# Cross-attention with eight heads and a mixture of experts on one core: another order of the attention steps on four engines

## Chip, cores and metric

The kernel runs on one core of a Trainium2 chip. The metric is the device time of one execution in microseconds (us). The kernel before was run three times: 2055.81, 2058.97 and 2060.05 us, median 2058.97 us. The profile is of one further execution, which took 2061.44 us.

## What is computed

16 batches of 224 tokens of width 512 attend to 750 context rows of width 384 each (8 heads of 64), and then go through a top-2 mixture of 8 experts. Cut to what matters:

```python
q = (layernorm(x) @ W_q).reshape(b, n, 8, 64)
k = (context @ W_k).reshape(b, j, 8, 64)
v = (context @ W_v).reshape(b, j, 8, 64)
sim = einsum('bihd,bjhd->bhij', q, k) * 64 ** -0.5
sim = where(mask[:, None, None, :], sim, -finfo.max)
x = x + einsum('bhij,bjhd->bihd', softmax(sim), v).reshape(b, n, 512) @ W_o + b_o
...
probs = softmax(layernorm(x) @ Wr); topk_probs, topk_experts = top_k(probs, 2)
for e in range(8):                       # at most 1120 tokens each
    y[idx_e] += gate_e * (relu(xe @ W1[e]) @ W2[e])
x = x + y
```

With these inputs only the last 192 keys of each batch can have the mask set, so the kernel takes the branch `attention_short`, which works on 192 keys.

## The kernel before

Matrix products are done with each operand split in two parts, "hi" and "lo": three matmuls (hi by hi, lo by hi, hi by lo) stand for one. What a matmul leaves in PSUM (its tiles are named ps...) is therefore read twice: the scalar engine (ACT) copies it rounded, the hi part, and then the vector engine (DVE) subtracts that from the same PSUM tile, the lo part. So a product that is an operand of another one takes the way TensorE (PE), ACT, DVE, PE.

`attention_short` goes through the 16 batches in eight pairs. The work of a pair is written as steps, a letter and a number each:

- `fx0` to `fx3` and `fc0` to `fc2`: turn 128 columns of the normalised tokens and of the context (L744, L748); `q0` to `q3`, `k0` to `k3`, `v0` to `v3`: the projections (L721; a q step has 12 matmuls of 448 columns, a k step 9 of 384, `v0` and `v3` 9 of 512, `v1` and `v2` 9 of 256).
- `s0` to `s15`: scores of one head and batch (L793, four matmuls into `psS`), then on DVE the mask and the row's largest value (L648), on ACT the exponential and its sum (L537). `u0` to `u15` on GpSimd (POOL): the reciprocal of the sum (L469) and the multiplication by it (L471).
- `t0` to `t15`: turn the probabilities (L802, L805 into `psT`), split them on ACT (L544) and DVE (L655). `o0` to `o15`: the product with v (L721 into `psO`); after each second one the split into `oT` (L548, L660).
- `wo0` to `wo3`: the output projection (L721), on DVE the residual addition and the statistics of the second layer norm (L624, L626, L628); `tl`: its reciprocal root on POOL (L455, L457); `ap`: its application (L632); `tt`: the turn of the result (L772, copy L678); `lg`, `lt`: router logits (L776, L830). `fs`, `fa`, `fl`, `fp`: the first layer norm of the next pair (L595, L602, L457, L608). `w10` to `w13`: the split of the output weights. `bi`: the bias (L482). `mb`: the next mask.

Each engine has its own list of steps, written out by hand in tables: `PE_FIRST`, `ACT_FIRST`, `DVE_FIRST`, `POOL_FIRST` for pair 0, `PE_STEPS` and its like for pairs 1 to 7, where a number below 0 (`t-3`, `o-4`) is a step of the pair before that is finished here, and `PE_END` and its like for what pair 7 leaves. [...]

Two rules of the waits matter below. All steps named in `RINGED` (q, k, v, fx, fc, wo, tt, lg) write the two PSUM tiles `psJ` in turn, in the order of PE's list; such a step waits until DVE is done with the one two places before it:

```python
at = ring(p, prev, nxt, kind, i)
if p is not None or at >= 2:
    pe.wait_ge(proj_done, at - 1)
```

And `s` has two PSUM tiles too: `s5` waits for DVE's mask step of `s3`. The same holds for `t` and, by pairs, for `o`. `s0` of a pair waits until every projection of the list before is split.

After the attention come the router and the choice of tokens (to about 640 us), then the experts' products to the end.

Of the kernel before, what the change touches and what calls it, by code (L numbers as in the profile page):

```python
# [191 lines left out]


DVE_STEPS = order("""
    s0 t-3 o-4 q1 s1 k1 t-2 fs0 fs1 t-1 o-3 v0 o-2 fs2 fs3 q2 o-1 s2 wo0 fa0 wo1 t0 s3 o0 v1
    s4 wo2 fp0 ap0 ap1 t1 v2 s5 v3 tt0 ap2 o1 t2 fp1 tt1 o2 fp2 s6 t3 wo3 t4 s7 k2 fp3 o3
    s8 ap3 o4 q3 t5 k3 s9 fc0 tt2 t6 tt3 s10 fx0 s11 t7 s12 fx1 o5 o6 lg0 t8 lt0 fx2 t9
    s13 fc1 fc2 t10 o7 fx3 s14 o8 s15 t11 o9 k0 mb0 o10 q0 t12 o11
""")
# [1727 lines left out]
```

## Time and profile before

| what | us |
| --- | --- |
| median of three runs | 2058.97 |
| the profiled execution | 2061.44 |
| its span, first to last instruction | 2059.7 |
| PE, DVE, ACT, POOL busy over the span | 1954.4, 1002.4, 719.4, 477.0 |
| start of the first `s0` | 35.99 |
| `s0` of pair 1, of pair 2, of pair 3 | 110.22, 174.86, 237.83 |
| last copy of the attention (logits) | 577.05 |

The span is in three parts. Up to 36 us inputs and weights are loaded and split. From there to 577 us runs the attention, and after it the router and the experts. The engines' busy time in a stretch is the length of their instructions without the overlaps; a line's idle time is what its engine waited just before it, with the instruction whose end released it. PE's instructions overlap: a matmul is shown for longer than it keeps the next one from starting, so that PE's pace is read from the distance between starts.

### The profile page before, as it was taken

The numbers are of one execution on the slowest core, as the hardware profiler recorded it, in microseconds if no ns is written. First come the engines' busy times: TensorE is split into PE (matmuls) and PEld (weight loads), VectorE is DVE, ScalarE is ACT, GpSimd is POOL, SyncE is SP. The second block draws the span as 40 slices with busy tenths as digits, with TensorE's granted clock in tenths as the row PEclk, the third lists the DMA queues.
The fourth block names the chain that finished last, engine by engine and source line by source line (L and its number), as shares of the span: only waits on it lengthen the run. The fifth ranks groups of instructions, "written<-read, shape, count | busy, mean of one in ns | idle before, by whom it ended". The sixth has DMA issues, their size and how long they took to land.

```text
span 2059.7 us, 30182 instructions
## 1 busy us (share of the span) xinstructions
PE 1954.4 (95%) x11419; PEld 1733.6 (84%) x11419; DVE 1002.4 (49%) x2471; ACT 719.4 (35%) x1928; POOL 477.0 (23%) x560
## 2 busy tenths in 40 slices
...
GB/s 210 19 52 53 87 87 74 66 53 36 54 142 144 16 118 123 15 52 145 45 15 57 139 46 16 105 120 31 28 141 73 16 112 113 31 21 162 32 5 27
DMA packets 96316, 148.40 MB, mean 72 GB/s; under 512 B 8608, under 2 KB 50096, under 8 KB 96160
## 3 DMA queue, kind: packets, MB, share of 16 engines
...
## 4 chain that ended last, share of the span: by engine, by line
PE 69%; DVE 1%; issue 1%; POOL 0%; POOLq 0%; ACT 0%; DVEq 0%
PE psH L1714 33%; PE psY L1714 31%; PE psY L1753 2%; PE psX L1728 1%; PE psI L1776 1%; DVE w_lo L1129 0%; PE psI L1766 0%; POOL out_dram L1498 0%; POOLq L1410 0%; DVE hT_lo L1688 0%; PE psI L1782 0%; DVE moves L1564 0%; DVE onehot L1572 0%; DVE slot_tile L1649 0%; DVE ys L1647 0%
## 5 line engine op out<-in xcount | busy, mean ns | idle before, releaser
L1688 DVE SCALAR_TENSOR_TENSOR hT_lo<-psH,hT_hi 128x384 fp32r<-128x384 f32 (+1 forms) x384 | 210.0, 547 | 867.3 <-ACT hT_hi L1528 527.9
L1528 ACT ACTIVATE hT_hi<-psH 128x384 fp32r<-128x384 f32 (+1 forms) x384 | 185.4, 483 | 1063.3 <-PE psH L1714 1063.3
L1714 PE MATMUL psH<-xgT_hi,w_hi 128*128 128x256 f32 (+3 forms) x1536 | 477.7, 311 | 9.6 <-issue 8.8
L1714 PE MATMUL psH<-xgT_hi,w_lo 128*128 128x256 f32 (+3 forms) x1536 | 476.6, 310 | 2.1 <-issue 2.1
L1714 PE MATMUL psH<-xgT_lo,w_hi 128*128 128x256 f32 (+3 forms) x1536 | 475.3, 309 | 1.7 <-issue 1.7
L1714 PE MATMUL psY<-w_hi,hT_hi 128*128 128x512 f32 (+1 forms) x921 | 371.7, 404 | 0.0
L1714 PE MATMUL psY<-w_lo,hT_hi 128*128 128x512 f32 (+1 forms) x921 | 362.7, 394 | 1.1 <-issue 1.1
L1714 PE MATMUL psY<-w_hi,hT_lo 128*128 128x512 f32 (+1 forms) x921 | 362.3, 393 | 0.0
L1714 PEld LDWEIGHTS psH<-xgT_hi,w_hi 128*128 128x128 f32 x1536 | 291.5, 190 | 35.3 <-issue 18.5
L1714 PEld LDWEIGHTS psH<-xgT_lo,w_hi 128*128 128x128 f32 x1536 | 291.7, 190 | 14.9
L1714 PEld LDWEIGHTS psH<-xgT_hi,w_lo 128*128 128x128 f32 x1536 | 291.4, 190 | 4.1 <-issue 4.1
L1487 POOL DMA_INDIRECT xg<-xn_rows,gid x72 | 71.5, 993 | 854.8 <-PE psX L1728 455.6
L1714 PEld LDWEIGHTS psY<-w_hi,hT_lo 128*128 128x128 f32 (+1 forms) x921 | 171.5, 186 | 41.1
L1498 POOL DMA_INDIRECT out_dram<-ys,sid x72 | 113.6, 1578 | 394.8 <-DVE ys L1620 380.2
L1714 PEld LDWEIGHTS psY<-w_lo,hT_hi 128*128 128x128 f32 (+1 forms) x921 | 172.5, 187 | 27.1 <-issue 1.4
L1714 PEld LDWEIGHTS psY<-w_hi,hT_hi 128*128 128x128 f32 (+1 forms) x921 | 172.2, 187 | 24.4 <-DVE hT_lo L1688 0.2
L1129 DVE TENSOR_TENSOR w_lo<-stage,w_hi 128x512 fp32r<-128x512 f32 x256 | 164.9, 687 | 2.6 <-ACT w_hi L1124 2.6
L1124 ACT ACTIVATE w_hi<-stage 128x512 fp32r<-128x512 f32 x256 | 146.6, 626 | 29.1 <-DMA stage<-in_L_ffn_W_dram 28.9
L469 POOL TENSOR_TENSOR rsum<-ssum,minus_one 112x2 f32<-112x2 f32 x128 | 91.1, 712 | 187.8 <-ACT probs L537 187.8
L537 ACT ACTIVATE probs<-probs,nmax 112x192 f32<-112x192 f32 x256 | 113.9, 450 | 41.8 <-DVE nmax L648 41.5
L471 POOL TENSOR_TENSOR probs<-probs,rsum 112x384 f32<-112x384 f32 x128 | 108.7, 849 | 10.0
L648 DVE CUSTOM_DVE_ANT_0 probs<-psS,mask_bias 112x192 f32<-112x192 f32 x256 | 80.0, 352 | 15.4 <-PE psS L793 14.5
...
## 6 DMA issues: line engine op xcount, KB each, us to landing
stage<-in_L_ffn_W_dram SPq DMA_DIRECT2D x128, 512.0 KB, 4.5
...
```

The costliest lines, as they stand in the source:

```text
L469: nc.gpsimd.tensor_tensor(rsum[:, i % 4, :], ssum[:, i % 4, :], T["minus_one"][0:R, :], ALU.pow).then_inc(recip, 1)
L471: nc.gpsimd.tensor_tensor(probs(i), probs(i), rsum[:, i % 4, :].unsqueeze(2).to_broadcast([R, 2, NKEY]), ALU.mult).then_inc(normed, 1)
L537: e = nc.scalar.activation(probs(i)[:, it, :], probs(i)[:, it, :], ACT.Exp, bias=nmax[:, i % 4, it:it + 1], scale=-1.0, accum_out=ssum[:, ...
L648: s = nc.vector.tensor_tensor_reduce(out=probs(i)[:, it, :], in0=psS[i % 2][0:R, it * NKEY:(it + 1) * NKEY], in1=mb[:, b, mask_order(half( ...
L1124: nc.scalar.activation(piece(T, 0, pair, j), staged(T, pair, j), ACT.Copy).then_inc(T["w_hi_done"], 1)
L1129: engine.tensor_tensor(piece(T, 1, pair, j), staged(T, pair, j), f32(piece(T, 0, pair, j)), ALU.subtract).then_inc(T["w_lo_done"], 1)
L1487: nc.gpsimd.indirect_dma_start(out=xg[0:m, t, :], out_offset=None, in_=A["xn2"], in_offset=bass.IndirectOffsetOnAxis(ap=gid[e % 2][0:m, c: ...
L1498: nc.gpsimd.indirect_dma_start(out=A["out"], out_offset=bass.IndirectOffsetOnAxis(ap=sid[e % 2][0:m, c:c + 1].bitcast(U32), axis=0), in_=y ...
L1528: h = nc.scalar.activation(hT[0][:, f % 2, 0:m], psH[f % 2][:, 0:m], ACT.Relu)
L1688: h = nc.vector.scalar_tensor_tensor(out=hT[1][:, f % 2, 0:m], in0=psH[f % 2][:, 0:m], scalar=0.0, in1=f32(hT[0][:, f % 2, 0:m]), op0=ALU. ...
L1714: mm = nc.tensor.matmul(out, stationary(a, c), moving(b, c), start=first and c == chunks[0] and j == 0, stop=last and c == chunks[-1] and ...
L1753: mm = nc.tensor.matmul(psY[t][0:2 * PART, :], hP[:, f % 2, :], w2[b][:, f, :], start=f == 0 and b == 0, stop=f == FCH - 1 and b == 1, ski ...
```

## The change

All eleven tables are written anew. Each table has the same steps as before, each once; no instruction of the attention is added or removed, none has another size, and no wait is written differently. What changes is the order in each engine's list, and with PE's list the order in which the two `psJ` tiles are given out. A line or two of the tables that are spoken of below:

```diff
 PE_STEPS = order("""
...
-    s6 s7 tt1 wo3 o2 t4 k2 o3 q3 t5 s8 k3 o4 t6 s9 s10 fc0 o5 tt2 t7 s11 tt3 fx0 o6 fx1 t8
...
+    wo3 t4 o3 k2 q3 s8 t5 s9 k3 o4 fx0 t6 s10 o5 tt2 t7 fx1 o6 tt3 s11 t8 s12 fc0 lg0 o7 fx2 t9 lt0 s13 o8 fc1 t10 fc2
...
 PE_FIRST = order("""
-    s0 s1 q1 s2 k1 v0 s3 t0 v1 s4 t1 o0 v2 s5 t2 o1 v3 q2 s6 t3 o2 k2 s7 t4 o3 q3 s8 t5 o4 k3
...
+    s0 v1 k1 s1 s2 q1 s3 v0 t0 v2 t1 s4 v3 o0 s5 t2 s6 o1 t3 k2 o2 s7 t4 o3 q2 q3 k3 t5 s8 o4 t6 fc0 s9 s10 o5 o6 t7 fc1
...
 ACT_FIRST = order("""
-    s0 s1 q1 s2 k1 v0 t0 s3 v1 t1 s4 o0 w10 v2 t2 s5 o1 w11 v3 q2 t3 s6 o2 w12 k2 t4 s7 o3 w13 q3 t5 s8 o4 k3
...
+    v1 k1 s0 s1 q1 w10 s2 v0 w11 s3 t0 o0 v2 w12 t1 v3 t2 s4 t3 k2 o1 s5 o2 t4 s6 o3 q2 q3 s7 t5 t6 k3 o4 w13 o5 s8 t7
...
-PE_END = order("t-3 o-4 t-2 o-3 wo0 t-1 o-2 wo1 o-1 wo2 tt0 wo3 tt1 tt2 tt3 lg0 lt0")
...
+    o-4 t-3 t-2 o-3 o-2 t-1 wo0 o-1 wo1 wo2 tt0 wo3 tt1 tt2 tt3 lg0 lt0
```

POOL's steady list moves `bi1` to `bi3` behind `u15`, its last normalisation.

Three places show what moves. The change is six lines longer, so its line numbers in this part of the program are six higher.

ACT in pair 0, behind the split of `q0` (`q_hi`, `k`, `va_hi`, `vb_hi` are splits of projections, `probs` the exponentials, `w_hi` the output weights). Before:

```order
L537 ACTIVATE probs,ssum<-probs,nmax 112x192 x4
L515 ACTIVATE q_hi<-psJ 64x448 x2
L517 ACTIVATE q_hi<-psJ 64x448 x2
L537 ACTIVATE probs,ssum<-probs,nmax 112x192 x2
L520 ACTIVATE k<-psJ 64x384
L522 ACTIVATE k<-psJ 64x256
L522 ACTIVATE k<-psJ 64x2x64
L508 ACTIVATE va_hi<-psJ 128x4x64
L509 ACTIVATE va_hi<-psJ 128x4x64
L544 ACTIVATE pT_hi<-psT 128x224
L537 ACTIVATE probs,ssum<-probs,nmax 112x192 x2
```

and now:

```order
L517 ACTIVATE vb_hi<-psJ 64x4x64
L518 ACTIVATE vb_hi<-psJ 64x4x64
L526 ACTIVATE k<-psJ 64x384
L528 ACTIVATE k<-psJ 64x256
L528 ACTIVATE k<-psJ 64x2x64
L543 ACTIVATE probs,ssum<-probs,nmax 112x192 x4
L521 ACTIVATE q_hi<-psJ 64x448 x2
L523 ACTIVATE q_hi<-psJ 64x448 x2
L533 ACTIVATE w_hi<-w_raw 128x512
L543 ACTIVATE probs,ssum<-probs,nmax 112x192 x2
L514 ACTIVATE va_hi<-psJ 128x4x64
L515 ACTIVATE va_hi<-psJ 128x4x64
```

The splits of `v1` and `k1` have moved ahead of the first two exponentials, and a weight split stands between `q1` and the third.

DVE in a steady pair, directly behind its split of `q3` (`pT_lo` is a t step, `k` the step `k3`, `L648 ISA` an s step, `cT_lo` is `fc0`, `xT_lo` is `fx0`, `x2T` is `tt2`). Before:

```order
L655 TENSOR_TENSOR pT_lo<-psT,pT_hi 128x448
L569 REGISTER_ALU
L586 TENSOR_TENSOR k<-psJ,k 64x384
L588 TENSOR_TENSOR k<-psJ,k 64x256
L590 TENSOR_TENSOR k<-psJ,k 64x2x64
L65 REGISTER_ALU
L648 ISA probs,nmax<-psS,mask_bias 112x192
L648 ISA nmax 112x1
L648 ISA probs,nmax<-psS,mask_bias 112x192
L648 ISA nmax 112x1
L569 REGISTER_ALU
L590 TENSOR_TENSOR cT_lo<-psJ,cT_hi 128x512
```

and now:

```order
L661 TENSOR_TENSOR pT_lo<-psT,pT_hi 128x448
L575 REGISTER_ALU
L592 TENSOR_TENSOR k<-psJ,k 64x384
L594 TENSOR_TENSOR k<-psJ,k 64x256
L596 TENSOR_TENSOR k<-psJ,k 64x2x64
L575 REGISTER_ALU
L596 TENSOR_TENSOR xT_lo<-psJ,xT_hi 128x448
L661 TENSOR_TENSOR pT_lo<-psT,pT_hi 128x224
L682 REGISTER_ALU
L684 COPY x2T<-psJ 128x4x112
```

The s step `s9` has gone ahead of `q3`, and the projection step that follows `k3` is `fx0` in place of `fc0`, with no s step between.

DVE at the very end, from `t-2` on (`pT_lo` are t steps, `oT_lo` the splits of attention outputs, `x_res`, `st`, `mv` a wo step, `xn` an ap step). Before:

```order
L655 TENSOR_TENSOR pT_lo<-psT,pT_hi 128x224
L660 TENSOR_TENSOR oT_lo<-psO,oT_hi 128x224
L624 TENSOR_TENSOR x_res<-psJ,x_res 112x512
L626 BN_STATS st<-x_res 112x6
L628 BN_AGGR mv<-st 112x2
L655 TENSOR_TENSOR pT_lo<-psT,pT_hi 128x448
L624 TENSOR_TENSOR x_res<-psJ,x_res 112x512
L626 BN_STATS st<-x_res 112x6
L628 BN_AGGR mv<-st 112x2
L660 TENSOR_TENSOR oT_lo<-psO,oT_hi 128x224
L632 TENSOR_SCALAR xn<-x_res,mv,rs 112x512
L624 TENSOR_TENSOR x_res<-psJ,x_res 112x512
```

and now:

```order
L661 TENSOR_TENSOR pT_lo<-psT,pT_hi 128x224
L666 TENSOR_TENSOR oT_lo<-psO,oT_hi 128x224
L661 TENSOR_TENSOR pT_lo<-psT,pT_hi 128x448
L630 TENSOR_TENSOR x_res<-psJ,x_res 112x512
L632 BN_STATS st<-x_res 112x6
L634 BN_AGGR mv<-st 112x2
L666 TENSOR_TENSOR oT_lo<-psO,oT_hi 128x224
L630 TENSOR_TENSOR x_res<-psJ,x_res 112x512
L632 BN_STATS st<-x_res 112x6
L634 BN_AGGR mv<-st 112x2
L638 TENSOR_SCALAR xn<-x_res,mv,rs 112x512
L630 TENSOR_TENSOR x_res<-psJ,x_res 112x512
```

The last turned probabilities (`t-1`) are split before `wo0` instead of behind it, and the last attention output (`o-1`) before `wo1` instead of behind it.

## Rows read from the trace of the kernel before

**Rows 1.** Windows: stretch, its length, busy time by engine, PEclk, DMA share, GB/s.

```profile
36.00:72.61 36.61, 28.47 (x148) 25.49 (x149) 18.27 (x59) 19.20 (x58) 12.38 (x16) 0.82 0.31 90
72.61:108.72 36.11, 29.06 (x174) 26.04 (x172) 22.81 (x74) 22.89 (x71) 19.62 (x23) 0.81 0.19 49
174.86:237.83 62.97, 61.87 (x409) 53.89 (x408) 52.64 (x160) 42.41 (x132) 33.91 (x48) 1.00 0.25 72
486.97:549.60 62.63, 57.80 (x377) 48.98 (x374) 43.92 (x140) 39.56 (x129) 35.62 (x48) 1.00 0.15 45
549.60:577.30 27.70, 21.20 (x89) 12.79 (x89) 11.97 (x24) 0.90 (x2) 4.66 (x10) 0.88 0.20 67
```

**Rows 2.** Timeline of PE in pair 0 and at its end: start, length, instruction, [idle before].

```profile
35.99 0.50 PE L793 MATMUL psS<-k,q_hi 128*112 128x192 f32 x1 [3.64 <-DVE q_lo L590]
...
37.60 0.63 PE L721 MATMUL psJ<-xT_hi,w_hi 128*128 128x448 f32 x1
...
42.13 0.36 PE L793 MATMUL psS<-k,q_hi 128*112 128x192 f32 x1
...
57.67 0.52 PE L721 MATMUL psO<-pT_hi,va_hi 128*128 128x224 f32 x1 [3.65 <-DVE vb_lo L590]
...
110.22 0.34 PE L793 MATMUL psS<-k,q_hi 128*112 128x192 f32 x1 [2.29 <-DVE q_lo L590]
```

**Rows 3.** Groups of ACT by line and form, 36 to 110 us: busy, mean ns | idle before.

```profile
L537 ACT ACTIVATE probs<-probs,nmax 112x192 f32<-112x192 f32 x32 | 14.3, 448 | 25.4 <-DVE nmax L648 25.4
L537 ACT ACTIVATION_READ_ACCUMULATOR probs<-probs,nmax 112x1 f32 x32 | 6.0, 187 | 0.0
L515 ACT ACTIVATE q_hi<-psJ 64x448 fp32r<-64x448 f32 x10 | 5.4, 536 | 4.4 <-PE psJ L721 4.3
L517 ACT ACTIVATE q_hi<-psJ 64x448 fp32r<-64x448 f32 x8 | 4.3, 540 | 0.1
L544 ACT ACTIVATE pT_hi<-psT 128x448 fp32r<-128x448 f32 x7 | 3.8, 542 | 0.1
...
L520 ACT ACTIVATE k<-psJ 64x384 fp32r<-64x384 f32 x4 | 1.9, 476 | 0.0
...
L508 ACT ACTIVATE va_hi<-psJ 128x256 fp32r<-128x256 f32 x2 | 0.8, 384 | 1.9 <-PE psJ L721 1.8
```

**Rows 4.** Groups of DVE by line and form, 36 to 110 us: the longest wait.

```profile
L582 DVE TENSOR_TENSOR q_lo<-psJ,q_hi 64x448 fp32r<-64x448 f32 x4 | 2.5, 616 | 11.8 <-ACT q_hi L517 11.8
```

**Rows 5.** Timeline of ACT: the ends of the steps k2 and q0 of pair 0.

```profile
72.06 0.55 ACT L522 ACTIVATE k<-psJ 64x256 fp32r<-64x256 f32 x2
...
107.63 1.09 ACT L517 ACTIVATE q_hi<-psJ 64x448 fp32r<-64x448 f32 x2
```

**Rows 6.** Waits of PE in a steady pair, 174.86 to 237.83 us: total, times, longest.

```profile
PE psO L721 <- DVE vb_lo L590: 0.7, 1, 0.7
```

**Rows 7.** Timeline of PE in a steady pair: q3, t5, fc0, tt2.

```profile
208.73 0.37 PE L721 MATMUL psJ<-xT_hi,w_hi 128*128 128x448 f32 x1
...
211.21 0.36 PE L802 MATMUL psT<-ident,probs 112*128 112x112 f32 x2
...
215.03 0.65 PE L748 MATMUL psJ<-ident,c_sb 128*128 128x128 f32 x4
...
216.91 0.60 PE L772 MATMUL psJ<-ident,xn 112*128 112x112 f32 x4 [0.38 <-DVE k L590]
```

**Rows 8.** Timelines of ACT and DVE at the same place: the split of q3.

```profile
211.41 1.09 ACT L515 ACTIVATE q_hi<-psJ 64x448 fp32r<-64x448 f32 x2 [0.84 <-PE psJ L721]
...
214.27 0.63 DVE L590 TENSOR_TENSOR q_lo<-psJ,q_hi 64x448 fp32r<-64x448 f32 x1
```

**Rows 9.** Timeline of PE in the tail, from wo0 on: the rows with a wait.

```profile
549.60 0.45 PE L721 MATMUL psJ<-w_hi,oT_hi 128*112 128x512 f32 x1 [0.96 <-DVE oT_lo L660]
...
558.31 0.45 PE L721 MATMUL psJ<-w_hi,oT_hi 128*112 128x512 f32 x1 [1.54 <-DVE oT_lo L660]
...
567.50 0.57 PE L772 MATMUL psJ<-ident,xn 112*128 112x112 f32 x4 [1.98 <-DVE xn L632]
```

More of the change, by code:

```diff
@@ L180 @@
 PE_STEPS = order("""
-    t-3 q1 s0 k1 o-4 t-2 o-3 s1 s2 t-1 v0 s3 q2 o-2 o-1 t0 wo0 wo1 s4 v1 wo2 t1 v2 o0 v3 s5 o1 tt0 t2 t3
-    s6 s7 tt1 wo3 o2 t4 k2 o3 q3 t5 s8 k3 o4 t6 s9 s10 fc0 o5 tt2 t7 s11 tt3 fx0 o6 fx1 t8
-    s12 lg0 o7 fx2 t9 lt0 s13 o8 fc1 t10 fc2 o9 t11 s14 fx3 s15 k0 q0 o10 o11 t12
+    q1 t-3 o-4 s0 k1 o-3 t-2 s1 s2 t-1 v0 s3 q2 o-2 t0 wo0 o-1 s4 v1 wo1 v2 t1 o0 s5 v3 wo2 t2 tt0 o1 s6 t3 tt1 s7 o2
+    wo3 t4 o3 k2 q3 s8 t5 s9 k3 o4 fx0 t6 s10 o5 tt2 t7 fx1 o6 tt3 s11 t8 s12 fc0 lg0 o7 fx2 t9 lt0 s13 o8 fc1 t10 fc2
@@ L184 @@
+    s14 o9 t11 s15 fx3 o10 t12 k0 q0 o11
 """)
 ACT_STEPS = order("""
-    o-4 t-3 q1 k1 t-2 o-3 s0 v0 t-1 o-2 q2 o-1 s1 t0 s2 v1 s3 o0 v2 t1 v3 o1 t2 s4 s5 t3 s6 o2 t4 k2 o3
-    s7 q3 t5 k3 s8 o4 fc0 t6 o5 t7 s9 fx0 fx1 t8 s10 s11 fx2 t9 o6 s12 fc1 fc2 o7 t10 t11 fx3 o8 o9
-    s13 k0 o10 s14 q0 o11 t12 s15
+    t-3 o-4 q1 k1 t-2 s0 o-3 o-2 s1 v0 t-1 q2 s2 o-1 t0 v1 v2 t1 s3 s4 v3 t2 t3 s5 o0 o1 s6 s7 o2 o3 t4 k2 q3 t5 o4 k3
+    fx0 t6 s8 s9 fx1 t7 s10 t8 o5 o6 s11 fc0 s12 o7 fx2 t9 fc1 fc2 t10 s13 t11 o8 fx3 o9 t12 s14 k0 q0 s15 o10 o11
@@ L191 @@
 """)
 DVE_STEPS = order("""
[L195 to L198, printed above, removed]
+    o-4 t-3 s0 q1 k1 s1 fs0 fs1 t-2 o-3 v0 fs2 s2 t-1 fs3 q2 wo0 o-2 o-1 s3 fa0 s4 v1 t0 wo1 fp0 v2 s5 fp1 ap0 ap1 v3 t1
+    o0 wo2 t2 tt0 fp2 tt1 t3 s6 s7 ap2 wo3 o1 t4 fp3 k2 o2 o3 ap3 s8 s9 q3 t5 k3 o4 fx0 t6 tt2 s10 fx1 tt3 s11 o5 s12 t7
@@ L199 @@
+    fc0 t8 lg0 lt0 fx2 t9 o6 s13 fc1 o7 t10 fc2 s14 fx3 o8 t11 k0 s15 t12 o9 q0 mb0 o10 o11
 """)
 POOL_STEPS = order("""
-    u0 fl0 u1 tl0 tl1 u2 u3 tl2 u4 u5 u6 tl3 u7 u8 u9 u10 u11 bi0 bi1 u12 u13 u14 bi2 bi3 u15
+    u0 u1 tl0 u2 fl0 tl1 u3 u4 tl2 u5 u6 tl3 u7 u8 u9 u10 u11 bi0 u12 u13 u14 u15 bi1 bi2 bi3
 """)
 PE_FIRST = order("""
-    s0 s1 q1 s2 k1 v0 s3 t0 v1 s4 t1 o0 v2 s5 t2 o1 v3 q2 s6 t3 o2 k2 s7 t4 o3 q3 s8 t5 o4 k3
-    s9 t6 fc0 o5 s10 t7 fc1 o6 fx0 s11 t8 o7 fc2 fx1 s12 t9 o8 fx2 s13 t10 o9 fx3 s14 t11 o10 k0 s15 t12 q0 o11
+    s0 v1 k1 s1 s2 q1 s3 v0 t0 v2 t1 s4 v3 o0 s5 t2 s6 o1 t3 k2 o2 s7 t4 o3 q2 q3 k3 t5 s8 o4 t6 fc0 s9 s10 o5 o6 t7 fc1
@@ L210 @@
+    s11 t8 o7 s12 t9 o8 s13 fx0 t10 o9 fx1 fc2 s14 fx2 t11 fx3 o10 k0 q0 t12 s15 o11
 """)
 ACT_FIRST = order("""
-    s0 s1 q1 s2 k1 v0 t0 s3 v1 t1 s4 o0 w10 v2 t2 s5 o1 w11 v3 q2 t3 s6 o2 w12 k2 t4 s7 o3 w13 q3 t5 s8 o4 k3
-    t6 s9 fc0 o5 t7 s10 fc1 o6 fx0 t8 s11 o7 fc2 fx1 t9 s12 o8 fx2 t10 s13 o9 fx3 t11 s14 o10 k0 t12 s15 q0 o11
+    v1 k1 s0 s1 q1 w10 s2 v0 w11 s3 t0 o0 v2 w12 t1 v3 t2 s4 t3 k2 o1 s5 o2 t4 s6 o3 q2 q3 s7 t5 t6 k3 o4 w13 o5 s8 t7
+    fc0 s9 t8 s10 fc1 o6 t9 o7 fx0 s11 t10 fx1 fc2 fx2 fx3 t11 s12 o8 k0 o9 s13 q0 t12 o10 s14 s15 o11
@@ L214 @@
 """)
 DVE_FIRST = order("""
-    s0 s1 q1 s2 k1 v0 s3 t0 v1 s4 t1 o0 w10 v2 fs0 fs1 s5 t2 o1 w11 v3 fs2 fs3 q2 fa0 s6 t3 o2 w12 k2 s7 t4 o3 w13 q3
-    fp0 fp1 s8 t5 o4 k3 fp2 fp3 s9 t6 fc0 o5 s10 t7 fc1 o6 fx0 s11 t8 o7 fc2 fx1 s12 t9 o8 fx2 s13 t10 o9 fx3 s14 t11 o10 k0
-    s15 t12 mb0 q0 o11
-""")
-POOL_FIRST = order("u0 u1 u2 u3 u4 u5 fl0 u6 u7 u8 u9 u10 u11 bi0 u12 bi1 u13 bi2 u14 bi3 u15")
-PE_END = order("t-3 o-4 t-2 o-3 wo0 t-1 o-2 wo1 o-1 wo2 tt0 wo3 tt1 tt2 tt3 lg0 lt0")
-ACT_END = order("t-3 o-4 t-2 o-3 t-1 o-2 o-1")
```

16 lines of the change are left out of this document (15 added, 1 removed).

## The prediction

> **What bounds the kernel now.** I read the windows first, then the waits and groups of lines of single stretches, and last PE's timeline at the places that the change touches. The windows [rows 1] show three different regimes in the attention, and the reader should keep them apart, because a new order is worth something else in each.
>
> In a steady pair PE is the bound: 61.87 of 62.97 us busy, the granted clock 1.00, and the only wait of length is 0.7 us for the split of `v2` [rows 6]; a second one, for `k3`, is the 0.38 before `tt2` [rows 7]. DVE is the next engine with 52.64 us.
>
> In pair 0 nothing is full. [...] What ACT waits for is one thing: 25.4 us before the exponentials, released by DVE's largest value [rows 3]. And DVE waits for ACT in turn, 11.8 us for the split of q [rows 4]. The two hand each other single steps. From the first `s0` to `s0` of pair 1 go 110.22 - 35.99 = 74.2 us [rows 2], although the pair has less work than a steady one.
>
> In the tail, from `wo0` at 549.60, PE waits again: 0.96 us for `o-3`, 1.54 us for `o-1`, 1.98 us for `xn` [rows 9].
>
> **The change part by part.** No instruction is added or removed and none has another size; transfers keep their place. Four terms.
>
> *Pair 0: -14 us.* Before, ACT splits `q1` right behind the first two exponentials. PE has its 12 matmuls from 37.60 to 42.13 [rows 2], that is 0.377 us each at the low clock or 0.84 ns a column, and ACT and DVE have nothing until it ends. Now `v1` and `k1` follow `s0`. I walk through the lists with the durations of the rows. PE: `s0` 36.0 to 36.8 (two s steps took 35.99 to 37.60), `v1` 9 x 0.215 (256 columns) to 38.7, `k1` 9 x 0.32 to 41.6, `s1` and `s2` to 43.2. ACT: `v1` from 38.9 (two copies of 0.38), `k1` (0.48 + 0.55) to 42.9, then both exponentials without a wait, 0.99 each, to 44.9; one such step is two of 448 ns and the 187 ns that read the sum, less overlap [rows 3]. The exponential of `s0` is 4.9 us later than before (42.9 against 38), and that costs nothing, since its reader `t0` now stands behind `q1`, `s3` and `v0` on PE, which last to 48. From there ACT has `q1` (2.2 us from 536 and 540), two weight splits, two exponentials, `v0` and six more splits of `t` (0.36 to 0.54) and `v`; it ends its `k2` at about 58.8. Before it was 72.61 [rows 5], with `s5`, `s6`, `q2` and `o1` done in addition, 1 + 1 + 2.2 + 0.35 = 4.5 us of ACT.
>
> The rest goes by fill. ACT's whole list up to its `q0` was 19.20 + 22.89 = 42.1 us; `s14` and `s15` now come behind `q0`, which leaves 40.3, of which 19.20 - 4.5 = 14.7 are done at 58.8. So 25.6 us remain. At the 63% of before they last 40.6 us and `q0` ends at 99.4; if ACT were as good as full (92%, what my walk without handover times gives), 27.8 us and 86.6. I take 75%, 34.1 us, `q0` at 92.9, because the q, k and v splits now stand in bunches with ready work between them. `s0` of pair 1 came 1.5 us behind ACT's `q0` (108.72 to 110.22), so it comes at 94.4: 15.8 us earlier, between 9.3 and 22.1. I take off 2 us, since each step passed between engines costs 0.05 to 0.2 us more than the walk has (from PE's end at 211.21 to ACT's start at 211.41 it is 0.2 [rows 7, 8]).
>
> *Pair 1: -1 us.* From `s0` of pair 1 to that of pair 2 it took 174.86 - 110.22 = 64.6 us, against 62.97 afterwards, so 1.7 us were lost to a late start. With `s14` and `s15` now left over for it, I expect 0.7 to remain. Ends 0 and -1.7.
>
> *Pairs 1 to 6: +2 us.* The wait for `v2` goes: `v3`, `wo2`, `t2` and `tt0` now stand between `v2` and `o1`. A new one comes. On `psJ` the step two places behind `q3` is now `fx0`. The split of `q3` needs, from PE's end at 211.21, 0.2 us to ACT, 2.2 there and 1.27 on DVE, to 214.90; `fc0` started at 215.03 [rows 7, 8]. Before, `t5`, `s8`, `k3`, `o4`, `t6`, `s9`, `s10` filled these 3.8 us with 0.13 to spare on the wrong side; now only `s8`, `t5`, `s9`, `k3`, `o4` do, one s step (0.8 us at the low clock, so 0.4) and `t6` (some 0.15) less, so PE waits 0.7 us. The wait for `k3` before `tt2` stays at about 0.2, and three places get close, each within 0.1 to 0.2: `s0` behind `q0`, `v0` behind `q1`, `lg0` behind `tt3`. Together 1.5 us against 1.23 (0.72 + 0.38 + 0.13), so +0.3 a pair, six times. Ends: -1.2 a pair if every wait goes, -7 us, and +1.2 if the new ones come on top, +7 us. All else that moves is covered by PE's full list.
>
> *Tail: -3.5 us.* `o-2` and `t-1` now run in the 0.96 us before `wo0`, which takes their matmuls, some 0.7 us, out from behind it; `t-1` can run there because POOL's `u15` no longer stands behind two bias additions. `o-1` runs before `wo1`, whose twelve matmuls hide its split, so 1.54 us go. The end of pair 7, which like pair 0 has no full engine (PE 57.80 of 62.63, with waits in it [rows 1]), I put at 1.2 us less, from the 4.8 us that PE is not busy there. The waits for `xn` stay, since the same chain of statistics, POOL and DVE precedes them. 1.54 + 0.7 + 1.2 = 3.4, rounded to 3.5. Ends 0 and -5.
>
> Sum: -14 - 1 + 2 - 3.5 = -16.5 us. Behind the attention the same work follows, shifted. The profiled execution took 2061.44 us, 2.5 above the median of the runs; 2061.44 - 16.5 = 2044.9 on its own, **2042.5 us** against the median of 2058.97.
>
> [...]
>
> [...]
>
> **Rivals.** About 0.2%, 4 us, is what a measurement of this kernel can tell from no change.
>
> - *Pair 0 fills better and the steady pairs tighten.* For it: every wait in pair 0 is a handover, none a full engine. Against: the q3 wait above. -20 - 1 - 3 - 4 = -28, 2031 us. Chance 0.15.
> - *The ping-pong of DVE and ACT goes on behind `k2`.* The exponentials still wait for DVE, since `s` has two PSUM tiles. At 63% and with 2 us lost in handovers pair 0 gives -7; with +2 and -2 in the tail, -7 in all, 2052. Chance 0.14.
> - *Slower: DVE becomes the bound in the steady pairs.* DVE has 52.64 of 62.97 us, and `s8` and `s9` now stand ahead of its split of `q3`. If they come late there, `fx0`, `k3`, `tt2` and `lg0` are late in turn, and PE idles each time. It decides from 16.5 + 2 = 18.5 over six pairs, 3.1 us a pair; at 4 us a pair it is 24 - 18.5 = +5.5, 2064.5. Against: before `q3` on DVE the walk has 0.15 us of slack, behind `lg0`, 3 us of matmuls, it recovers. Chance 0.06.
> - *The lists move, but the same handovers remain.* Little of pair 0 can then be gained and the rest cancels: 2058. Chance 0.03.
> [...]
>
> **How the numbers follow.** My forecast has the chance 0.61, with 2035 to 2049 from the ends of pair 0 (-9 to -20) set against the likely 2 us either way of the others. The range of 2031 to 2053 takes in the first two rivals and leaves out about 0.1 to 0.15. Faster by over 0.2%: 0.61 + 0.15 + 0.01 and most of the second rival, 0.13, make 0.90. Within 0.2%: 0.01 of it and the fourth, 0.04. Slower: 0.06.
>
> **What would show it.** Right: `s0` of pair 1 starts at 92 to 99 us, ACT's wait for DVE in pair 0 falls from 25.4 us to under 15, a steady pair takes 62.5 to 64 us with a wait of 0.5 to 1 us before `fx0`, and no wait for `oT` before `wo2`. Wrong: a steady pair over 65 us, or `s0` of pair 1 behind 102 us.

## The result, and the profile after

The change makes the kernel faster by more than predicted: 2025.9 us (median of 4 runs, 2023.94 to 2027.68) against 2057.39 us for the kernel before on the same chip (4 runs, 2054.96 to 2060.05). The ratio is 0.9835, with an interval of 0.981 to 0.9859: 34 us less, 29 to 39. Run once more beside other kernels it took 2027.39 us, ratio 0.985 [0.9837, 0.9864]. The range of 2031 to 2053 does not hold: the direction was right, the size too small.

The profiled execution has a span of 2026.0 us, 33.7 less than before. To see where they went, both attentions are cut at points that both lists have: the first `s0`, the first matmul of `wo0` in each pair, that of the tail, and the last copy of the logits (us, from the starts on PE's timeline and the start of DVE's last copy).

| | before | after | difference |
| --- | --- | --- | --- |
| first `s0` | 35.99 | 35.48 | -0.5 |
| from there to `wo0` of pair 1 | 86.28 | 63.50 | -22.8 |
| `wo0` of pair 1 to `wo0` of pair 7 | 377.85 | 371.15 | -6.7 |
| `wo0` of pair 7 to `wo0` of the tail | 49.48 | 47.97 | -1.5 |
| from there to the last copy | 27.45 | 24.63 | -2.8 |
| the rest of the span | 1482.65 | 1483.27 | +0.6 |

Two thirds lie in pair 0, most of them ahead of `s0` of pair 1. PE's timeline after, at the first `s0`, at `s0` of pair 1 and at its `wo0`, answers to [rows 2]:

```profile
35.48 0.50 PE L799 MATMUL psS<-k,q_hi 128*112 128x192 f32 x1 [3.63 <-DVE q_lo L596]
...
89.36 0.34 PE L799 MATMUL psS<-k,q_hi 128*112 128x192 f32 x1
...
98.98 0.46 PE L727 MATMUL psJ<-w_hi,oT_hi 128*112 128x512 f32 x1
```

`s0` of pair 1 starts 20.9 us earlier than at 110.22, and without the wait of 2.29 us that stood before it.

Windows of the change (columns as in [rows 1]): pair 0, a steady pair from `wo0` to `wo0`, pair 7 and the tail:

```profile
36.00:90.00 54.00, 48.98 (x327) 44.58 (x327) 42.56 (x135) 42.60 (x132) 27.07 (x34) 0.98 0.31 88
160.89:222.73 61.84, 61.46 (x412) 53.59 (x410) 52.31 (x160) 41.99 (x132) 34.00 (x46) 1.00 0.25 73
470.13:518.10 47.97, 46.00 (x302) 38.49 (x301) 35.50 (x113) 29.60 (x99) 27.21 (x39) 0.98 0.20 59
518.10:543.00 24.90, 20.15 (x84) 12.29 (x82) 12.05 (x24) 0.90 (x2) 5.34 (x10) 0.90 0.22 74
```

Pair 7 takes the steady tables without the steps that prepare a next pair (`OF_NEXT` in the kernel); PE is busy 46.00 us in its stretch, where a steady pair has 61.46.

and the first of these stretches before:

```profile
36.00:90.00 54.00, 40.79 (x213) 36.10 (x214) 30.12 (x95) 28.94 (x88) 17.93 (x22) 0.78 0.21 61
```

In the same 54 us ACT now works 42.60 us in place of 28.94, DVE 42.56 in place of 30.12, and PE's granted clock is 0.98 where it was 0.78. What is gone is ACT's wait for DVE's largest value. Groups of ACT after, 36 to 90 us, which hold as many exponentials as [rows 3] had in 74 us:

```profile
L543 ACT ACTIVATE probs<-probs,nmax 112x192 f32<-112x192 f32 x32 | 14.1, 446 | 0.0
L543 ACT ACTIVATION_READ_ACCUMULATOR probs<-probs,nmax 112x1 f32 x32 | 6.1, 191 | 0.0
L521 ACT ACTIVATE q_hi<-psJ 64x448 fp32r<-64x448 f32 x9 | 4.8, 538 | 1.2 <-PE psJ L727 1.2
...
L550 ACT ACTIVATE pT_hi<-psT 128x448 fp32r<-128x448 f32 x7 | 3.8, 539 | 1.6 <-PE psT L811 1.5
```

The 25.4 us before the exponentials are 0.0. What is left are waits for PE, 12.8 us in all that the view of waits lists, where before it listed 31.5. A third of them is one wait at the start, for the matmuls of `v1`, where ACT waited for the first largest value before (3.3 of the 25.4 us), so this part changed its name more than its length:

```profile
ACT vb_hi L517 <- PE psJ L727: 4.4, 1, 4.4
```

DVE's counterpart, the 11.8 us for q [rows 4], has become the second of the next two groups, and the largest of DVE's waits is now the one for PE in the first:

```profile
L654 DVE CUSTOM_DVE_ANT_0 probs<-psS,mask_bias 112x192 f32<-112x192 f32 x32 | 10.0, 351 | 4.1 <-PE psS L799 4.0
...
L588 DVE TENSOR_TENSOR q_lo<-psJ,q_hi 64x448 fp32r<-64x448 f32 x4 | 2.5, 614 | 2.1 <-ACT q_hi L523 2.1
```

ACT's timeline at the two ends that [rows 5] gave (its `k2`, its `q0`):

```profile
56.19 0.54 ACT L528 ACTIVATE k<-psJ 64x256 fp32r<-64x256 f32 x2
...
86.17 1.09 ACT L523 ACTIVATE q_hi<-psJ 64x448 fp32r<-64x448 f32 x2
```

They end at 56.73 and 87.26 us; predicted were 58.8 and 92.9. In a steady pair, all that the view of waits lists for PE between 160.89 and 222.73 us is one wait before `fx0`, for the split of `q3`, 0.36 us long on the timeline; the 0.7 for `v2` [rows 6] and the 0.38 before `tt2` [rows 7] are no longer listed:

```profile
PE psJ L750 <- DVE q_lo L596: 0.4, 1, 0.4
```

In the tail `wo0` starts without a wait at 518.10, and PE's timeline has three waits from there to `xn`, none of them for a split of `oT` [rows 9]; a second wait for `xn`, 0.68 us before, is gone too:

```profile
528.84 0.48 PE L727 MATMUL psJ<-w_hi,oT_hi 128*112 128x512 f32 x1 [0.40 <-DVE x_res L630]
...
532.65 0.60 PE L778 MATMUL psJ<-ident,xn 112*128 112x112 f32 x4 [0.40 <-DVE x_res L630]
...
535.29 0.57 PE L778 MATMUL psJ<-ident,xn 112*128 112x112 f32 x4 [2.04 <-DVE xn L638]
```

### The profile page after: what moved, and what is told of

Its sections match the earlier page's. It is cut to its first block, busy times and chain, and to the rows that moved or that the text cites. A ratio compares the mean times of both kernels' runs of the same rounds, so it can differ in the third digit from the quotient of the medians.

```text
span 2026.0 us, 30188 instructions
## 1 busy us (share of the span) xinstructions
PE 1940.2 (96%) x11419; PEld 1722.4 (85%) x11419; DVE 1000.5 (49%) x2471; ACT 715.7 (35%) x1928; POOL 476.6 (24%) x560
## 4 chain that ended last, share of the span: by engine, by line
PE 70%; DVE 1%; issue 1%; POOL 0%; POOLq 0%; ACT 0%; DVEq 0%
PE psH L1720 34%; PE psY L1720 32%; PE psY L1759 2%; PE psX L1734 2%; PE psI L1782 1%; DVE w_lo L1135 0%; PE psI L1772 0%; POOL out_dram L1504 0%; DVE hT_lo L1694 0%; POOLq L1416 0%; ACT hT_hi L1534 0%; PE psI L1788 0%; DVE moves L1570 0%; DVE onehot L1578 0%; DVE slot_tile L1655 0%
```

## Experiments

All times are medians; ratios are to the kernel before, run beside them on the same chip (2056.96, 2058.62 and 2058.89 us in three groups of runs, 17, 29 and 17 executions). Microseconds behind a ratio are its distance from 1 times that median, with the ends of its interval.

### The three stages apart

Three kernels take the new tables of one stage each and keep the old ones elsewhere.

```diff
e1_first:   PE_FIRST, ACT_FIRST, DVE_FIRST, POOL_FIRST of the change
e2_steady:  PE_STEPS, ACT_STEPS, DVE_STEPS, POOL_STEPS of the change
e3_end:     PE_END, ACT_END, DVE_END of the change
```

> Only the four tables of pair 0 are new, the steady ones and the end are those of before. Theory 1 (the three parts add up, each by its own stage): 21 to 24 us less than before, s0 of pair 1 starts at 89 to 91 us, the steady pair stays at 62.97 us. Rival (pair 0 gains only because the new steady lists take over what it leaves, s14, s15 and late splits): 12 to 18 us less, and pair 1 takes 2 us or more over a steady one.

> Only the four steady tables are new. Theory 1: the waits before o1 and tt2 are gone, the one before fx0 is 0.4 us, a pair takes 61.9 us; six pairs give 6.5 us and pair 7 about 1.5, so 7 to 8 us less than before. Rival (the steady lists gain only behind the new pair 0): the pair stays within 0.3 us of 62.97 and the time within 2 us of before.

> Only the three tables of the end are new. Theory 1: the 1.54 us before wo2 are gone and the matmuls of o-2 and t-1 stand before wo0; 2 to 3 us less than before. Rival (POOL's u15 stands behind two bias additions in the old steady list, so t-1 comes late and holds wo0): no gain or up to 1 us more.

| | time, us | ratio | pair 0 | a steady pair | pair 7 and tail |
| --- | --- | --- | --- | --- | --- |
| before | | | 86.28 | 62.97 | 76.93 |
| e1_first | 2038.93 | 0.9907 [0.989, 0.9924], -19.1 us | 64.67 | 62.99 | 77.25 |
| e2_steady | 2047.35 | 0.9946 [0.993, 0.9962], -11.1 us | 83.08 | 61.86 | 74.42 |
| e3_end | 2058.25 | 1.0004 [0.9995, 1.0014] | 82.61 | 62.97 | 75.18 |
| the change | 2025.9 | 0.9835 [0.981, 0.9859], -34 us | 63.50 | 61.86 | 72.60 |

Pair 0 is from its first `s0` to `wo0` of pair 1, pair 7 and tail from `wo0` of pair 7 to the last copy. Each stage becomes shorter where its tables are new and almost only there, so the stages can be judged one by one. Pair 0 is the part that was forecast too small, and the steady pairs the part with the wrong sign.

`e1_first` gave 19.1 us (15.6 to 22.6), less than the 21 to 24 of its theory. The rival's sign is absent all the same: `s0` of pair 1 starts at 89.70, and from there to `s0` of pair 2 it takes 63.1 us, 0.1 over a steady pair and not 2. `e2_steady` gave 11.1 us (7.8 to 14.4), more than the 7 to 8 expected, with the pair of 61.9 us that was expected.

The tail is 1.75 us shorter in the profile of `e3_end`, but the total shows nothing of it: 0.8 us more than before, from 1.0 less to 2.9 more, so that the 2 to 3 us of its theory did not come and the rival's "no gain" did. Its own executions lie between 2050 and 2061.7 us. `e11_end_pool` below takes the question up.

One thing stands beside the argument: pair 0 with its old lists took 86.28 us in the profile of before and 82.6 to 83.1 in those of `e2_steady` and `e3_end`, with the granted clock at 0.90 in place of 0.82 from 36 to 110 us in the latter. `e7_o1_later` and `e11_end_pool`, with the same lists of pair 0, have 86.23 and 84.08 us. So one profile of this stage is good to some 4 us, and the total times have to speak for the rest.

### Pair 0: its opening or its rest

```diff
e5_opening, the first nine steps in the new order, the rest in the old:
-PE    s0 s1 q1 s2 k1 v0 s3 t0 v1 | s4 t1 o0 v2 s5 t2 ...
+PE    s0 v1 k1 s1 s2 q1 s3 v0 t0 | s4 t1 o0 v2 s5 t2 ...
e6_rest, the first nine in the old order, the rest as in the change:
-PE    s0 s1 q1 s2 k1 v0 s3 t0 v1 | s4 t1 o0 v2 s5 t2 ...
+PE    s0 s1 q1 s2 k1 v0 s3 t0 v1 | v2 t1 s4 v3 o0 s5 ...
```

ACT and DVE are cut in the same way; POOL's list is new in the second only.

> The kernel before; in pair 0 only the first nine steps s0 s1 q1 s2 k1 v0 s3 t0 v1 stand in the new order (PE: s0 v1 k1 s1 s2 q1 s3 v0 t0, ACT and DVE likewise), the rest as before. Theory of the prediction (the opening breaks the exchange of single steps, the rest only fills better): 5 to 8 us less than before. Rival (the opening only moves the wait to v2 or o1, and the order behind it brings the gain): 0 to 3 us less.

> The other half: in pair 0 the first nine steps as before, all behind them in the new order; steady pairs and end as before. If opening and rest add up to the 21 us of pair 0: 13 to 16 us less than before. If the rest brings nearly all: 18 us or more less. If it needs the opening to keep TensorE's granted clock up: under 10 us less and a clock under 0.9 from 36 to 90 us.

The opening alone: 2055.29 us, 0.9979 [0.9968, 0.9989], -4.3 us (-6.6 to -2.3). The rest alone: 2042.57 us, 0.9917 [0.99, 0.9934], -17 us (-20.6 to -13.6). Both together gave -19.1 in `e1_first`, so they nearly add up. Both lie between what the two theories expected. The waits tell more than the totals. ACT's group in `e5_opening`, 36 to 104 us:

```profile
L533 ACT ACTIVATE probs<-probs,nmax 112x192 f32<-112x192 f32 x32 | 14.3, 447 | 17.7 <-DVE nmax L644 17.7
```

and ACT's longest wait in `e6_rest`, 35.5 to 92 us (total, times, longest), with its window:

```profile
ACT probs L535 <- DVE nmax L646: 6.9, 3, 3.2
```

```profile
36.00:90.00 54.00, 46.40 (x309) 41.78 (x308) 39.77 (x130) 40.19 (x120) 25.33 (x32) 0.97 0.31 89
```

The opening takes 7.7 of the 25.4 us of waiting away, the rest 18.5, with only three waits left, all at the old opening. The third theory for `e6_rest`, that it needs the opening to keep the granted clock up, is out: the clock is 0.97 without it. The long stretch of old order behind the ninth step is where most of the time was, not the start that the prediction walked through.

### Is it DVE's order that makes the ping-pong?

In the old lists DVE has most mask steps (`s`) behind a projection split that ACT has to copy first. So ACT copies, DVE subtracts, DVE masks, and only then has ACT its exponential: one works while the other waits. The trace of before shows it at `q1` and `s2`. The last of PE's four matmuls of `s2` starts at 42.55 and is shown for 0.26 us, and yet DVE, whose list has `q1` first, waits 5.97 us for ACT's split of `q1`, subtracts from 44.60 and masks `s2` from 45.88; ACT waits 2.00 us for that and starts the exponential of `s2` at 46.57. If that is the cause, DVE's list alone must remove most of it. `e9_dve_order` is the kernel before, with each such `s` of DVE in pair 0 ahead of the split that it followed; PE, ACT and POOL keep their old lists. Four of these steps (`s5`, `s6`, `s8`, `s9`) also pass layer-norm steps that stood between, and `s10` passes `o5`.

```diff
 DVE_FIRST = order("""
-    s0 s1 q1 s2 k1 v0 s3 t0 v1 s4 t1 o0 w10 v2 fs0 fs1 s5 t2 o1 w11 v3 fs2 fs3 q2 fa0 s6 t3 ...
+    s0 s1 s2 q1 k1 s3 v0 t0 s4 v1 t1 o0 w10 s5 v2 fs0 fs1 t2 o1 w11 v3 fs2 fs3 s6 q2 fa0 t3 ...
```

> The kernel before; only DVE's list of pair 0 is new: each s step stands one place further ahead, in front of the projection split that it followed. PE, ACT and POOL keep their lists. Theory (ACT and DVE hand each other single steps because DVE has the mask step behind the split that it gets from ACT): ACT's wait for the largest value falls from 25.4 to under 14 us and the time by 8 to 14 us, half or more of what pair 0 gives in all. Rival (PE's order and the opening are what counts): under 4 us, the wait moves to the splits of q and k on DVE.

2044.92 us, 0.9942 [0.9926, 0.9957]: -12 us (-15.2 to -8.9), inside the 8 to 14 expected. Pair 0 takes 72.19 us in place of 86.28. ACT's groups, 36 to 97 us, DVE's wait for the split of q, and the window:

```profile
L535 ACT ACTIVATE probs<-probs,nmax 112x192 f32<-112x192 f32 x32 | 14.2, 446 | 6.4 <-DVE nmax L646 6.2
...
L513 ACT ACTIVATE q_hi<-psJ 64x448 fp32r<-64x448 f32 x10 | 5.4, 540 | 6.2 <-PE psJ L719 6.1
```

```profile
DVE q_lo L580 <- ACT q_hi L515: 3.7, 4, 1.0
```

```profile
36.00:90.00 54.00, 45.45 (x281) 41.13 (x281) 37.88 (x122) 38.93 (x120) 26.80 (x33) 0.90 0.26 74
```

The wait for the largest value falls from 25.4 us to 6.2, and DVE's wait for the split of q in turn from 11.8 to 3.7. What ACT waits for next is PE (6.1 us for q), which still has its old list. No engine has less work, so it was the order of one engine that held the others, for 12 of the 19.1 us that pair 0 gives in all; the other 7 needed the other lists too. Not all of it need be handover: the layer-norm steps that DVE did between a split and the mask step take 3.7 us on the timeline of before (1.29, 0.38, 1.00 and 1.00), and the run moves them out of ACT's way together with the splits.

### Or is it PE's clock?

Another theory says that PE is granted a lower clock because it idles, so that matmuls in pair 0 take longer, and that the gain is the clock's. Matmuls do take longer there: the twelve of `q1` in pair 0 start 0.377 us apart [rows 2] at a granted clock of 0.50 (window 37.60 to 42.13 us), the twelve of `q3` in a steady pair, as wide, 0.207 us apart [rows 7] at 1.00 (208.73 to 211.21 us). `e8_keep` is the kernel before with 83 additional matmuls of a block of zeros, added to running `psO` sums, where PE waited in pair 0. They add work and no change of order.

```diff
+KEEP = {("o", 1): (28, 0), ("o", 3): (16, 1), ("fc", 0): (18, 0), ("o", 5): (10, 0), ("fx", 0): (7, 1), ("o", 7): (4, 1)}
...
+                    if not prev and (kind, i) in KEEP:
+                        n, at = KEEP[kind, i]
+                        for _ in range(n):
+                            nc.tensor.matmul(psO[at][:, 0:128], T["zrow"][:].bitcast(F32R), T["w_hi"][:, 1, 0:128], start=False, stop=False,
+                                             skip_group_check=True)
```

> The kernel before, with 83 extra matmuls of 128 columns by a block of zeros in PE's waits of pair 0 (before o1, o3, fc0, o5, fx0, o7), added onto o tiles that are still being summed, so they change no result. If the low granted clock causes a good part of the slow pair 0: the clock from 57 to 100 us rises from about 0.8 to over 0.9 and the time falls by 3 to 8 us. Rival (the clock only follows the waits; splits and handovers set the pace): the clock rises and the time stays within 1.5 us of before, or the extra matmuls add 1 to 2.

2056.63 us, 0.9986 [0.9974, 0.9997]: -2.9 us (-5.3 to -0.6). The window from 57 to 79 us, before:

```profile
57.00:79.00 22.00, 18.04 (x97) 16.10 (x97) 13.10 (x38) 12.27 (x34) 7.42 (x9) 0.87 0.00 1
```

and with the additional matmuls, with ACT's exponentials from 36 to 104 us:

```profile
57.00:79.00 22.00, 21.25 (x152) 19.85 (x150) 13.98 (x43) 14.09 (x41) 7.88 (x10) 1.00 0.00 1
```

```profile
L540 ACT ACTIVATE probs<-probs,nmax 112x192 f32<-112x192 f32 x32 | 14.3, 447 | 24.8 <-DVE nmax L651 24.8
```

In this window the clock went from 0.87 to 1.00 and from 57 to 100 us from 0.77 to 0.92, as expected. ACT waited as long as before (24.8 against 25.4 us). The gain of 2.9 us lies between the 3 to 8 of the one expectation and the 1.5 of the other, and its interval reaches into both. Nor is it the whole of the clock: from 36 to 90 us it is 0.91 here, 0.78 before and 0.98 in the change, and whether the additional matmuls hold real ones back was not traced. What speaks more clearly is a comparison at the same clock. `e8_keep` from 36 to 90 us:

```profile
36.00:90.00 54.00, 47.42 (x313) 43.98 (x313) 32.47 (x103) 32.03 (x98) 20.09 (x25) 0.91 0.20 57
```

`e9_dve_order` has 0.90 there. Pair 0 takes 82.49 us in the one and 72.19 in the other: at an equal clock DVE's order alone makes 10 us, more than the 4 by which profiles of the same lists differ. So most of the gain is not the clock's, which rises with the order by itself (0.78 before, 0.90 with DVE's new order); how much of the rest is, these runs don't say to better than a few us.

### The steady pairs

`e7_o1_later` takes the kernel before and moves two steps ahead of `o1` on PE, so that only the wait for `v2` goes. `e4_fx0_later` and `e10_tt2_later` take the change and move the steps that are still waiting.

```diff
 e7_o1_later (from before, PE_STEPS)
-    v3 s5 o1 tt0 t2 t3 s6 s7 tt1
+    v3 s5 t2 s6 o1 tt0 t3 s7 tt1
 e4_fx0_later (from the change, PE_STEPS)
-    o4 fx0 t6 s10 o5 tt2 t7 fx1
+    o4 t6 s10 fx0 o5 tt2 t7 fx1
 e10_tt2_later (from the change, PE_STEPS)
-    o4 fx0 t6 s10 o5 tt2 t7 fx1
+    o4 t6 s10 fx0 o5 t7 tt2 fx1
```

> The kernel before with t2 and s6 ahead of o1 in PE's steady list, nothing else. If a steady pair is PE's own work plus its waits: 0.5 of the 0.72 us before o1 go, a pair takes 62.5 us, 2.5 to 3.5 us less in all. Rival (DVE or ACT paces the pair and the waits of PE only show it): the wait turns up at tt0 or behind, a pair stays at 62.9 to 63.0.

> The changed kernel with t6 and s10 moved ahead of fx0 in PE's steady list alone. If the wait before fx0 is what still costs in a steady pair: it falls from 0.4 to under 0.1 us, a pair takes 61.5 us in place of 61.88, and the time is 2 to 2.5 us under that of the changed kernel. Rival (DVE paces the pair behind q3, so the wait only moves to tt2 or lg0): the pair stays at 61.8 to 61.9 us.

> The changed kernel with t6 and s10 ahead of fx0 and t7 ahead of tt2 in PE's steady list. If the 0.4 us behind q3 and k3 are a wait for the chain of the two splits alone: now neither fx0 nor tt2 waits, a pair takes 61.5 us in place of 61.88, 2 to 2.5 us less than the changed kernel. Rival (DVE's chain behind k3 moves the wait once more, to fx1 or lg0): 61.8 to 61.9 us a pair.

| | a steady pair, us | PE's listed waits in it | time, us | ratio |
| --- | --- | --- | --- | --- |
| before | 62.97 | `v2` 0.7, `tt2` 0.4 | | |
| e7_o1_later | 62.36 to 62.42 | `tt2` 0.4 | 2056.68 | 0.9988 [0.9978, 0.9998] |
| the change | 61.77 to 61.91 | `fx0` 0.4 | 2027.39 | 0.985 [0.9837, 0.9864] |
| e4_fx0_later | 61.84 to 61.90 | `tt2` 0.4 | 2026.65 | 0.9841 [0.9825, 0.9858] |
| e10_tt2_later | 61.75 to 61.85 | none | 2027.94 | 0.9851 [0.9838, 0.9864] |

`e7_o1_later` does what was expected of it: the pair falls by 0.6 us as the wait of 0.7 goes, and the kernel by 2.5 us (0.4 to 4.5). The waits of a pair in `e7_o1_later` and in `e4_fx0_later`:

```profile
PE psJ L770 <- DVE k L588: 0.4, 1, 0.4
```

```profile
PE psJ L776 <- DVE k L594: 0.4, 1, 0.4
```

In `e4_fx0_later` the wait for `q3` went and the one for `k3` came back at `tt2` with the same length; the pair stays, as the rival to my expectation had it. `e10_tt2_later` removes that one too, and the view of waits lists nothing for PE. Its window of one pair:

```profile
163.00:224.77 61.77, 61.77 (x410) 53.66 (x410) 52.27 (x160) 41.93 (x132) 34.01 (x46) 1.00 0.26 73
```

PE is shown busy in all of the 61.77 us, 0.1 less than the change; 61.5 were expected. Since a matmul is shown for longer than it holds up the next (those of `q3` in the kernel before for 0.36 to 0.37 us, with 0.207 from start to start), small gaps between starts don't appear in this figure, and where the other 0.3 us went the listed waits don't show. Neither kernel can be told from the change in time: these two orders win nothing more, and whether another would was not tried.

### The tail, with POOL's part

`e11_end_pool` is `e3_end` with POOL's `u15` ahead of two bias additions (the change moves a third, `bi1`, behind it).

```diff
 POOL_STEPS = order("""
-    ... u11 bi0 bi1 u12 u13 u14 bi2 bi3 u15
+    ... u11 bi0 bi1 u12 u13 u14 u15 bi2 bi3
```

> The kernel before with the three tables of the end, and POOL's u15 ahead of bi2 and bi3. If the end by itself gave little because t-1 waited for u15 behind two bias additions: from wo0 of pair 7 to the last copy it is 3 to 3.5 us less than before (76.93 us), against 1.75 less with the end's tables alone. Rival (u15 is late for another reason, ACT's s15 at the end of its old steady list): 1.5 to 2 us less, as with the end alone.

2054.32 us, 0.9985 [0.9974, 0.9996]: -3.1 us (-5.3 to -0.8), and 73.83 us from `wo0` of pair 7 to the last copy, 3.1 less than before, inside the 3 to 3.5 expected, where `e3_end` had 1.75. The waits for splits of probabilities ahead of `wo0` are the same in both runs, 1.24, 0.93 and 1.10 us. What differs is `t-1` behind them, which reads what `u15` leaves. The last of the three waits, POOL's multiplication of `u15` and `t-1` in `e3_end`:

```profile
541.97 0.56 PE L727 MATMUL psO<-pT_hi,va_hi 128*128 128x224 f32 x1 [1.10 <-DVE pT_lo L661]
...
543.41 0.83 POOL L477 TENSOR_TENSOR probs<-probs,rsum 112x384 f32<-112x384 f32 x1
...
544.29 0.63 PE L808 MATMUL psT<-ident,probs 112*128 112x112 f32 x2
```

and in `e11_end_pool`, with `wo0` of the tail:

```profile
545.19 0.83 POOL L477 TENSOR_TENSOR probs<-probs,rsum 112x384 f32<-112x384 f32 x1
...
546.21 0.37 PE L727 MATMUL psO<-pT_hi,va_hi 128*128 128x224 f32 x1 [1.10 <-DVE pT_lo L661]
...
547.31 0.36 PE L808 MATMUL psT<-ident,probs 112*128 112x112 f32 x2
...
548.10 0.46 PE L727 MATMUL psJ<-w_hi,oT_hi 128*112 128x512 f32 x1 [0.24 <-DVE oT_lo L666]
```

In `e3_end` `u15` ends at 544.24 and `t-1` starts 0.05 us later; in `e11_end_pool` `u15` has been over for 1.3 us when `t-1` starts. From the last of the three waits to `wo0` it is 3.01 us in the first and 1.89 in the second. The totals (0.8 us more against 3.1 less) point the same way: POOL's move and the new end belong together. That `u15` is the reason is likely and not proven: in these 3.01 us the granted clock was 0.50 in `e3_end`, in the 1.89 us 1.00, and the slower matmuls alone, 0.21 us apart in place of 0.11, would have kept `t-1` until about 544.0.

### The change once more

> The changed kernel itself, beside e10 on the same chip: 30 to 34 us less than before; a steady pair of 61.8 to 61.9 us.

2027.39 us, 0.985 [0.9837, 0.9864], in the same group as `e9_dve_order`, `e10_tt2_later` and `e11_end_pool`: -30.9 us (-33.7 to -28.1). Its profile has 64.99 us for pair 0, 371.30 for the six steady pairs and 71.19 for pair 7 and the tail, within 1.5 us each of the first. ACT's `k2` and `q0` in it:

```profile
57.79 0.54 ACT L528 ACTIVATE k<-psJ 64x256 fp32r<-64x256 f32 x2
...
87.75 1.09 ACT L523 ACTIVATE q_hi<-psJ 64x448 fp32r<-64x448 f32 x2
```

They end at 58.33 and 88.84, both 1.6 us later than in the first profile, and `s0` of pair 1 starts at 90.94. The granted clock from 36 to 46 us is 0.71 here and was 0.88 there.

## Why the prediction was right in kind and wrong in size

**Pair 0: mechanism right, term too small by 7 us.** That ACT and DVE hand each other single steps, and that this and no full engine sets the length, is what `e9_dve_order` shows for 12 of the 19.1 us, less what the layer-norm steps have in it. The step that failed is "I take 75%", with the 2 us taken off behind it. No row gave the 75%; it was chosen between 63, which is ACT's 22.89 of 36.11 us [rows 1], and 92. From the end of `k2` to the end of `q0` it took 87.26 - 56.73 = 30.5 us, where 75% gave 34.1: 3.6 us. ACT was busy 25.1 us of it (25.6 forecast), a fill of 82%. The 2 us for handovers did not come on top. Single ones are as short as they were put: 0.06 us from the end of DVE's split of q at 35.93 to the first `s0` at 35.99, 0.13 from the end of its `k3` at 216.78 to `tt2` at 216.91, and the 0.2 that the prediction names. Against that, `s0` came 2.1 us behind ACT's `q0`, not 1.5. So the step was 5.0 us too small. The other 2.1 us lie ahead of it: `k2` ended at 56.73, where the walk had 58.8. In all 2.1 + 3.6 + 2.0 - 0.6 = 7.1, and `s0` of pair 1 started at 89.36, where 94.4 + 2 = 96.4 had been forecast.

The other profiles tell the two apart. In the five with the new lists of pair 0 (the change twice, `e1_first`, `e4_fx0_later`, `e10_tt2_later`) `k2` ends between 56.73 and 58.84, so the walk had it right within what executions differ by; from there to the end of `q0` it takes 30.5 to 30.6 us in each. So the 2.1 us vary, and the fill of 75% was too low in every one of them. As far as a cause can be named, the handovers were counted twice: the fill was put below the walk's 92%, which has no handovers in it, and then they were subtracted again. The 92% would have been no better founded: from the measured `k2` it gives 84.5 for `q0`, 2.7 us early.

The emphasis was off too. The walk treated the opening step by step and the rest by one share; `e5_opening` and `e6_rest` put 4 us into the opening and 17 into the rest.

**Pair 1: -1 forecast.** From `s0` of pair 1 to that of pair 2 it takes 151.43 - 89.36 = 62.1 us, against 64.6 before. 1.1 of these 2.5 us is the steady pair's own gain, 1.4 the lost start; 0.2 remains of the 0.7 that were expected to.

**Steady pairs: +2 forecast, -6.7 measured.** This is the second step that failed, by 8.7 us, and the only one with the wrong sign. The count of waits was 1.5 new for 1.23 old. Of the old ones `v2` went, as said. Of the new ones only the wait for `q3` came, at 0.36 us where 0.7 was forecast. The 0.4 us for an s step in that sum holds in the trace of before: `s9` takes 0.45 us there, from 214.05 to 214.50, at a granted clock of 1.00, and the first `s0` and `s1` take 1.6 us together at 0.50. The wait of `k3` before `tt2`, "stays at about 0.2", is no longer listed, since PE reaches `tt2` later by what it waits at `fx0`; `e4_fx0_later` shows the two as one wait that moves. And the three places called close, at 0.1 to 0.2 each, cost nothing that the trace lists. So 1.23 became 0.36, which is 0.87 of the 1.12 us that a pair gained; the other 0.25 stand in no listed wait, and where they lie was not traced. A close place had been priced as if it were a wait in every pair; the range had the right end in it, -1.2 a pair.

**Tail: -3.5 forecast, -4.3 measured** for pair 7 and the end together, by the steps that were named: `wo0` without its 0.96 us, no wait for `oT` at the 1.54, POOL's `u15` as the likely condition (`e11_end_pool`), the first wait for `xn` unchanged (2.04 against 1.98). That the second one, 0.68 us, would go had not been counted.

**Sum.** Forecast -14 - 1 + 2 - 3.5 = -16.5. Measured by the same cuts: -20.9 for `s0` of pair 1, 0.5 of it an earlier first `s0`; -1.4 for pair 1's start; -6.7; -4.3; +0.6 behind the attention: -32.7, to which the 1.1 of the steady gain that pair 1 makes ahead of its `wo0` is to be added: -33.8, where the spans differ by 33.7.

**The rivals.** The first one, pair 0 fills better and the steady pairs tighten, with chance 0.15 and 2031 us, is what happened, and by 5 us too little of it. I held the `q3` wait against it, which is there and half as long. Its two parts are independent, and both came at their good end. The second, the ping-pong goes on, is refuted by ACT's wait of 0.0. The third, DVE as the bound of the steady pairs, is refuted by their 61.84 us, in which DVE's 52.31 hold PE for 0.4. The fourth would have left the waits where they were.

For the 0.01 in the sum of the chances, 1988 us, no run shows the term: it was an estimate that a steady pair could shrink by 62.97 - 53.89 = 9.1 us, to the busy time of PE's weight loads [rows 1]. What the runs showed is that the share of these loads rose from 53.89 of 62.97 us to 53.59 of 61.84, and that `e10_tt2_later` has PE busy in all of 61.77 us with 53.66 us of loads: the 8 us between are no room that these orders of steps find, and they are not made of listed waits that another order takes away. The starts leave little room either. Half of the 0.377 us between the matmuls of `q1` at a clock of 0.50 is 0.19, and those of `q3` had 0.207 at 1.00 already. If the pace goes with the clock, which is an estimate from these two, at most a tenth of such a step was to be gained.

**What would show it.** Of the four signs, ACT's wait under 15 us and no wait for `oT` came true. `s0` of pair 1 came ahead of its 92 to 99 (89.36), and a steady pair is shorter than its 62.5 to 64 (61.8), with 0.36 us before `fx0` and not 0.5 to 1.
